# Attention heads: reciprocals of row sums taken for two row tiles at a time, and the steps of a unit reordered by pairs of tiles

## The reference, cut to what matters

```python
    def _L0_attn_ref(x, w_qkv, w_out):
        qkv = (x @ w_qkv.T).reshape(B, S, 3 * H, D)
        q = qkv[:, :, :H]
        k = qkv[:, :, H:2 * H]
        v = qkv[:, :, 2 * H:]
        scale = 1.0 / jnp.sqrt(jnp.asarray(D, dtype=x.dtype))
        logits = jnp.einsum('bqhd,bkhd->bhqk', q, k) * scale
        weights = jax.nn.softmax(logits.astype(jnp.float32), axis=-1).astype(logits.dtype)
        combined = jnp.einsum('bhqk,bkhd->bqhd', weights, v).reshape(B, S, H * D)
        return combined @ w_out.T
    x = x + _layernorm(_L0_attn_ref(_layernorm(x, axis=-1), L0_attn_w_qkv, L0_attn_w_out), axis=-1)
```

## Time and profile before

| what | value |
|---|---|
| median of three runs | 926.19 us (923.75 to 926.33) |
| span of the profiled execution | 923.3 us |
| PE busy | 832.7 us, 90% |
| DVE busy | 766.5 us, 83% |
| ACT busy | 605.9 us, 66% |
| POOL busy | 430.6 us, 47% |

### The profile page before, as it was taken

The page is one execution under the profiler, slowest core; times in us unless marked ns, Lnnn a source line. Parts: engine busy times, 40 slices in busy tenths (PEclk is TensorE's granted clock), DMA queues, the critical chain, the costliest instruction groups (busy, mean ns, idle before and its releaser), DMA issues.

```text
span 923.3 us, 13156 instructions
## 1 busy us (share of the span) xinstructions
PE 832.7 (90%) x4330; PEld 534.6 (58%) x4330; DVE 766.5 (83%) x1597; ACT 605.9 (66%) x1042; POOL 430.6 (47%) x455
## 2 busy tenths in 40 slices
PE   3889999999999999989899998679788999998997
PEld 2555665665665565655565565457555555554686
DVE  3788999889989999999899998585598687876637
ACT  5677767777777676766667767374545767657531
POOL 3134354354445277787667771171323434433301
PEclk9999999999999999999999999799989999999999
DMA  3388858966977667857857668130000000000001
GB/s 122 78 184 156 143 117 190 163 126 136 206 134 153 130 131 144 166 110 144 157 103 132 136 130 159 24 106 0 1 1 1 1 0 2 0 2 1 1 1 45
DMA packets 276867, 86.29 MB, mean 93 GB/s; under 512 B 267584, under 2 KB 272448, under 8 KB 276416
## 3 DMA queue, kind: packets, MB, share of 16 engines
q1 hardware_dynamic: 275520, 80.05, 44.8%
q0 software_dynamic: 992, 5.34, 1.9%
q10 hardware_dynamic: 288, 0.07, 0.0%
HBM read 17.29 MB, written 1.05 MB: 20 GB/s over the span
## 4 chain that ended last, share of the span: by engine, by line
PE 40%; DVE 37%; issue 9%; ACT 8%; DMA 3%; POOL 1%; SPq 1%; POOLq 0%; DVEq 0%; ACTq 0%
DVE EP L1762 9%; DVE nmax L1747 8%; PE ps L1097 7%; PE ps L1099 7%; PE ps L1098 7%; PE ps L1120 4%; DVE ptm L1861 3%; PE ps L1358 3%; PE ps L1344 3%; PE ps L1135 3%; PE ps L1323 3%; DVE ps L1947 2%; DMA ET<-EP 2%; DVE OL L1821 2%; DVE st L1661 1%
## 5 line engine op out<-in xcount | busy, mean ns | idle before, releaser
L1523 ACT ACTIVATE EP<-ps,rinv 128x1024 f16<-128x1024 f32 x128 | 142.2, 1112 | 44.5 <-DVE rinv L1757 42.9
L1762 DVE SCALAR_TENSOR_TENSOR EP<-ps,rinv,EP 128x1024 f16<-128x1024 f32 x128 | 163.3, 1276 | 2.4 <-ACT EP L1523 2.0
L1513 ACT ACTIVATE ps<-ps,nmax 128x1024 f32<-128x1024 f32 x128 | 139.2, 1088 | 35.7 <-DVE nmax L1747 35.2
L1747 DVE TENSOR_REDUCE nmax<-ps 128x1 f32<-128x1024 f32 x128 | 155.0, 1211 | 0.7 <-PE ps L1099 0.7
L1097 PE MATMUL ps<-KH,QH 128*128 128x512 f32 x256 | 115.4, 451 | 8.3 <-DVE KL L1729 4.2
L2106 POOL TENSOR_TENSOR wgu<-wgu,ptm 128x688 f32<-128x688 f32 x60 | 99.7, 1661 | 45.8 <-DVE ptm L1861 43.7
L1097 PE MATMUL ps<-ET,VH 128*128 128x512 f16 x256 | 98.7, 385 | 17.8 <-DMA ET<-EP 14.2
L1099 PE MATMUL ps<-KH,QL 128*128 128x512 f32 x256 | 100.8, 394 | 0.0
L2106 POOL TENSOR_TENSOR wdn<-wdn,ptm 128x512 f32<-128x512 f32 x45 | 57.7, 1282 | 92.2 <-DVE ptm L1861 91.0
L1098 PE MATMUL ps<-KL,QH 128*128 128x512 f32 x256 | 100.5, 392 | 0.0
L1098 PE MATMUL ps<-ET,VH 128*128 128x512 f16 x256 | 98.3, 384 | 0.0
(11 more groups left out here) (250 smaller groups left out, 2126.7 us busy)
## 6 DMA issues: line engine op xcount, KB each, us to landing
wqr<-in_wqk SPq DMA_DIRECT2D x16, 256.0 KB, 3.6
wgu<-in_tern POOLq DMA_DIRECT2D x3, 1024.0 KB, 6.1
wvr<-in_wv SPq DMA_DIRECT2D x8, 256.0 KB, 3.9
wor<-in_wo SPq DMA_DIRECT2D x16, 128.0 KB, 3.1
ET<-EP SPq DMA_TRANSPOSE x128, 4.3
X<-in_x SPq DMA_DIRECT2D x2, 512.0 KB, 5.7
prw<-in_down_idx POOLq DMA_DIRECT2D x2, 256.0 KB, 7.0
tern<-in_l_wuq_rep SPq DMA_DIRECT2D x1, 512.0 KB, 4.5
```

The costliest lines, as they stand in the source:

```text
L1513: e.activation(bank, bank, ACT.Exp, bias=nmax[:, c:c + 1], scale=1.0, accum_out=rsum[:, c:c + 1]).then_inc(exped.sem, 1)
L1523: e.mul(EP[:, n % NE_RING, 0, :], SB(u, j), rinv[:, c:c + 1]).then_inc(e_hi.sem, 1)
L1747: e.tensor_reduce(nmax[:, c:c + 1], SB(u, j), AX.X, ALU.max, negate=True).then_inc(maxed.sem, 1)
L1762: e.scalar_tensor_tensor(out=EP[:, n % NE_RING, 1, :], in0=SB(u, j), scalar=rinv[:, c:c + 1], in1=EP[:, n % NE_RING, 0, :], op0=ALU.mult, ...
```

## The change

First, `row_inv` now stands for two tiles: it waits for the exponentials of tile j and scales and inverts two columns, j-1 and j, in one operation each. It is called for j = 1 and j = 3 alone, so a unit has two steps i in place of four. Both tiles of the pair get their high part only after it.

Second, the tables. `i1` covers tiles 0 and 1 of unit u+1, and `i3` tiles 2 and 3 of unit u. Therefore h2 and l2, which stood at the end of a round for unit u+1, now stand near the beginning of the next round (there for unit u). The tables themselves:

```diff
-    order = ("i3 f0 F0 h3 A7 M0 l3 S0 p0 e0 X0 x0 i0 h0 M1 e1 S1 x1 O0 y0 l0 S2 X1 o0 i1 p1 w1 y1 w0 h1 S3 M2 "
-             "p4 A0 A1 X2 A2 A3 l1 p2 e2 x2 i2 A4 M3 A5 A6 h2 y2 l2 w2 p3 e3").split()
+    order = ("f0 F0 A7 S0 M0 i3 h2 e0 l2 S1 p0 X0 x0 h3 l3 M1 e1 S2 x1 O0 y0 X1 i1 h0 l0 S3 o0 p1 w1 y1 w0 h1 M2 "
+             "p4 A0 A1 X2 A2 A3 l1 p2 e2 x2 A4 M3 A5 A6 y2 w2 p3 e3").split()
...
-                todo.append(({"i": "row_inv", "h": "cast_e", "l": "rest_e"}[what], u if j == 3 else u + 1, j))
+                todo.append(({"i": "row_inv", "h": "cast_e", "l": "rest_e"}[what], u if j > 1 else u + 1, j))
...
             elif what == "row_inv":
+                for j in (at[1] - 1, at[1]):
+                    sum_down.at[at[0], j] = sum_down.n + 1
+                    inverted.at[at[0], j] = inverted.n + 1
                 sum_down.mark(*at)
                 inverted.mark(*at)
...
-                    c = 4 * (u % 2) + j
+                    c = 4 * (u % 2) + j - 1
                     w.wait_ge(*exped[u, j])
                     if u >= 2:
                         w.wait_ge(*e_lo[u - 2, j])
-                    e.tensor_scalar(rsc[:, c:c + 1], rsum[:, c:c + 1], 1.0 / E_UP, None, ALU.mult).then_inc(sum_down.sem, 1)
+                    e.tensor_scalar(rsc[:, c:c + 2], rsum[:, c:c + 2], 1.0 / E_UP, None, ALU.mult).then_inc(sum_down.sem, 1)
                     w.wait_ge(*sum_down[u, j])
-                    e.reciprocal(rinv[:, c:c + 1], rsc[:, c:c + 1]).then_inc(inverted.sem, 1)
+                    e.reciprocal(rinv[:, c:c + 2], rsc[:, c:c + 2]).then_inc(inverted.sem, 1)
```

More of the change, by code:

```diff
@@ L130, in project @@
         return [(what, *at), (what + "_hi", *at), (what + "_lo", *at)]
-    before = ("t0 t1 n0 n1 n2 n3 k0 K0 n4 n5 n6 T0 Q0 v0 n7 T1 X0 x0 y0 Q1 X1 y1 X2 y2 x1 x2 x3 e0 v1 h0 S0 M0 "
-             "v2 y3 e1 X3 x4 S1 i0 v3 M1 X4 S2 v4 e2 l0 M2 i1 i2 y4 x5 M3 S3 X5 y5 h2 l2 l1 h1 X6 X7 e3 y6 y7 "
+    before = ("t0 t1 n0 n1 n2 n3 k0 K0 n4 n5 n6 T0 Q0 v0 n7 T1 X0 x0 y0 Q1 X1 y1 X2 y2 x1 x2 x3 e0 v1 S0 M0 "
+             "v2 y3 e1 X3 x4 S1 v3 M1 X4 S2 v4 i1 h0 l0 M2 h1 e2 y4 x5 l1 S3 M3 X5 y5 X6 X7 e3 y6 y7 "
              "x7 x6").split()
@@ L162, in order_of_heads @@
     loads = []
-    order = ("i3 f0 F0 h3 A7 M0 l3 S0 p0 e0 X0 x0 i0 h0 M1 e1 S1 x1 O0 y0 l0 S2 X1 o0 i1 p1 w1 y1 w0 h1 S3 M2 "
-             "p4 A0 A1 X2 A2 A3 l1 p2 e2 x2 i2 A4 M3 A5 A6 h2 y2 l2 w2 p3 e3").split()
-    last = ("f0 o0 w3 i3 A7 O0 L0 h3 l3 L1 F0 L2 L3 A0 L4 A1 A2 A3 w5 A4 L5 L6 L7 A5 A6 w4").split()
+    order = ("f0 F0 A7 S0 M0 i3 h2 e0 l2 S1 p0 X0 x0 h3 l3 M1 e1 S2 x1 O0 y0 X1 i1 h0 l0 S3 o0 p1 w1 y1 w0 h1 M2 "
+             "p4 A0 A1 X2 A2 A3 l1 p2 e2 x2 A4 M3 A5 A6 y2 w2 p3 e3").split()
+    last = ("f0 o0 w3 i3 A7 O0 L0 h2 l2 h3 l3 L1 F0 L2 L3 A0 L4 A1 A2 A3 w5 A4 L5 L6 L7 A5 A6 w4").split()
     end = ("F0 o0 A7 U0 f0 O0 O1 U1 o1").split()
```

## The result

The kernel after takes 1420.94 us, the median of four runs (1420.24 to 1421.95), against 926.26 us for the kernel before beside it (four runs, 923.75 to 928.67). The ratio is 1.5342, with a 95% interval of 1.5306 to 1.5377. The prediction was 1315 us with a range up to 1395 us: slower, as predicted, but by 495 us and not 389.

What follows compares the result with a forecast made beforehand. PE and DVE were taken as nearly equally full in a 17.25 us unit. To the span of 923.3 us, waits added 293 us and the clock 96 us: 1312 us, 1315 us as the runs' median, range 1200 to 1395 us.

Steps and rivals of the forecast that it cites:

- The pace of before and what the change removes: A unit takes 17.25 us, PE and DVE nearly equally full; 16.6 us of DVE go, but the saving is hidden.
- the fourth rival: Start of each round: DVE sets the pace, PE's waits are filled, some 10 us come back, 916 us; chance 0.04.
- The three waits: In PE's queue, three scores steps a unit wait for the low part, 4.2, 3.35 and 3.35 us.
- The sum of 27.0 us a round: PE's own work of 16.1 us a unit plus waits of 4.2, 3.35 and 3.35 us, against 17.25 us before.
- The order of matmuls: PE keeps program order; if matmuls could overtake, a projection would fill part of the first wait, some 40 us less.
- The clock: PE's clock falls at two of three gaps a round, 1.55 us each: 3.1 us a unit, 96 us in all.
- The second rival: PE's clock stays down longer, through the steps between two waits: +10 us a unit, about 1500 us; chance 0.05.
- The ends: Parts behind the heads take the same 329 us; the last two full rounds, lacking projections, grow by 7 and 3 us.
- What would show it: In the heads: F's starts 28 to 31 us apart, DVE's share about 0.6, PE's clock 0.75 to 0.95.

## Why the prediction was right in sign and too low, step by step

**The pace of before and what the change removes** were right in kind: the saving is hidden by the new waits, as the same round of 34.11 and 34.12 us with and without it shows. The rule of thumb behind the fourth rival (10 us of 16.6 come back) is not borne out: 23 us less of DVE brought 4 us, and the 10 us between the order with single operations and the kernel after lie in the clock. Two columns cost 0.16 and 0.17 us against 0.15 and 0.16 us: as good as nothing, as taken. Over the whole kernel after that holds (0.18 us in the mean), but with one pair, and with both at their best order, the scaling of two columns took 11 to 12 us longer in all, as its long ones end with POOL's operations.

**The three waits** were right. Predicted were 4.2, 3.35 and 3.35 us, 10.9 a round; the round shown has 4.06, 3.10 and 3.10 us, each some 0.16 us longer from the end at which the next matmul could have started, 10.7 in all. They number 92 for about 90, and each has been undone by itself and given 153 to 173 us. The sum of 27.0 us a round was right as well: 27.15 us were measured in the round at full clock, with the gaps filled.

**The order of matmuls.** X0 did not overtake the waiting S1: in the round shown, with S1's first matmul at 419.53, the projection's first one is at 422.25 us.

**The clock** is the step that failed. It was put at "two falls of three at 1.55 us, 3.1 us a unit". The 28 full rounds take (1022.36 - 78.73) / 28 = 33.70 us by the starts of F, that is 6.7 us above the 27.0 us of the waits. In the round shown, the burst behind the first gap takes 4.26 us from start to start (from 419.53 us; the projection's last matmul starts at 423.57 and takes 0.22) against 2.69 us at the full clock, +1.57; S2, O0 and X1 some 6.9 us against 1.38 + 1.42 + 1.31 = 4.11, +2.8; and the third burst (S3, eight A, X2 and S0) 12.2 us against 9.27, +2.95. These are 7.3 us.

How often the clock fell can't be read from the first matmul of S alone. In the timeline of PE from 79 to 1029 us there are 85 gaps at S. Behind 72 of them the first matmul has 0.76 to 0.80 us, and the clock is down. Behind 13 it has 0.50 us, but at 10 of these the clock fell 0.4 to 1.3 us later, within the same burst. One such, and one of the three behind which it stayed up:

```profile
237.33 0.50 PE L1100 MATMUL ps<-KH,QH 128*128 128x512 f32 x1 [3.01 <-DVE EP L1765]
...
238.37 0.60 PE L1101 MATMUL ps<-KL,QH 128*128 128x512 f32 x1
...
270.94 0.50 PE L1100 MATMUL ps<-KH,QH 128*128 128x512 f32 x1 [3.10 <-DVE EP L1765]
```

From 238.37 us the distances between starts go from 0.23 to 0.39 and 0.43 us; behind 270.94 us they stay at 0.22 to 0.24 us. The three gaps without a fall (270.94, 563.76 and 571.25 us) lie in two rounds, which take 31.9 and 29.5 us from F to F, while the other full rounds, with three falls each, take 32.0 to 36.4 us.

So two things were too small. The clock fell behind 82 of 85 gaps, 2.9 of the three in a round and not two, which at 1.55 us would be 1.4 us a round more. And it came back later: in the round shown after 3.2 us behind the first gap, which cost the 1.57 us that the earlier trace rows had shown, but only after 5.9 us behind the second and third, at 2.8 and 2.95 us each. By 6.7 / 2.9 a fall cost 2.3 us in the mean. That two gaps filled brought 145 us, that one gap filled brought 58.5 us, and that the round of 34.11 us takes 27.15 us at full clock, show that this time was the clock's, and not an error in the waits.

The second rival had this mechanism ("the clock stays down longer, through the steps between two waits", +10 us a unit, some 1500 us). The measured case lies between it and the forecast, with 6.7 us. I gave it 0.05 and ended the range at 1395 us, since one row had the clock back after 3.3 us, and here one burst in three did the same. The rule of "TensorE: Matmul & The Clock Gate", section "HAM oscillation — how this bites in real kernels", in the Trainium skill, was right on how often the clock falls here (82 of 85); worked out at 1.55 us a fall it gave 1360 us, 60 us short, because of the price.

**The ends.** One of the 29 rounds with 9.75 us of waiting and 3.1 us of clock lies ahead of the first F, so that the forecast has about 13 us there; it took 18.8 us, with gaps of its own in round 0 and in the steps ahead of it. The parts behind the heads took 329.1 us, for "the same 329 us". By the account, the miss of 106 us is 102 in the 31 units (477.7 for 376), 6 in the start, and the rest rounding and what lies around the span.

**What would show it.** F's starts lie 32.7 us apart in the mean, above the 28 to 31; DVE's share is 0.49 and not 0.6, both off with the longer round. The clock of 0.77 lies inside the 0.75 to 0.95, near its lower end. ACT's wait for PE before x grew, to 143.4 us at QH alone.

**What stays open.** With all three waits undone the two pairs still cost 117 us, and one pair 56. For the one pair DVE's waits and the longer scalings are about as large as the loss. For both pairs they are seen (47.2 and 55.4 us, and some 12 us in the length of the scalings) but were not taken away one at a time, and PE's own 40 waits of 45.1 us are mixed in. That kernel also differs from the one after in PE's order, so 380 us is not the pure sum of the three single edits (483 us); how much of the gap between the two is that, and how much is that a second wait is partly hidden by a first, was not tried.

## What to carry to other kernels

A step in a fixed order costs little by its own time and much by what stands between it and the engine that waits: walk from the end of the last matmul ahead of a wait to the next one, through every queue, before you move a step behind another engine's work. Merging two tiny operations makes both users wait for the later producer; where the engines are all nearly full, that wait is dearer than the operation, and removing an operation outright (here a scaling folded into a constant, 4 us) has no such wait. Price a gap that recurs in PE by its length and by the clock behind it, from several bursts like those that will follow it, not from one lone gap. And read a whole burst before you say that the clock stayed up: it can fall behind the first matmuls.

## What the runs showed of the hardware

- In the round shown of the kernel after, the bursts behind gaps of 3.1 to 4.1 us ran at a granted clock of 0.63, 0.58 and 0.76, and lost 1.6, 2.8 and 2.95 us; the full clock was back 3.2, 5.9 and 5.9 us behind the burst's start. Why the first differs was not tried.
- The length of a gap alone did not decide on the clock. With all three gaps of a round unfilled the clock fell behind 82 of 85, 10 of these 0.4 to 1.3 us after the burst had begun at full clock; where two of three were filled, it fell behind 17 of 32, and the gaps of 3.01 to 3.10 us lie on both sides. In the kernel before, 2.44 us fell and 2.74 us did not the earlier trace rows. What decides was not tried.
- A lone gap of 4.1 us in a round of 24 us cost 2.0 us a round by the clock. Idle matmuls into a bank that is overwritten anyway took it away: 58.5 us less with 17, 30 us less with 8.
- Tiny DVE operations of one or two columns took 0.13 to 0.17 us each, but for those of the next point. A scaling and the reciprocal that waits for it took 0.26 us up to the next operation, two that don't need each other 0.12 us. 23 us less of DVE's load brought 4 us and 16 us more cost 7 to 9 us, though DVE was busy for 94 to 98% of the stretch.
- The scaling of a tile of 128x2 ran on until a POOL operation beside it had ended, and so took up to 1.64 us: with one pair 15 of 32 took over 0.3 us, and 14 of these end 0.02 to 0.03 us behind a POOL operation; with both pairs at their best order it was 15 of 64, 14 of them so. The same operation on 128x1 never took over 0.16 us, though 40 of 128 started while POOL was at work. The reciprocal behind it stayed at 0.17 us on two columns. Why the two differ was not tried.
